# Expert outputs of a mixture-of-experts layer: the last expert's rows kept in a buffer of their own, the other pairs summed during its sends

## What is computed

```python
x = x + _L0_attn_ref(_layernorm(x), ...)
x = x + _L0_ffn_ref(_layernorm(x), Wr, W1, b1, W2, b2, fw1, fb1, fw2, fb2)   # 8 experts, top 2, capacity 1.25
x = x + _L1_attn_ref(_layernorm(x), ...)
x = x + _L1_ffn_ref(_layernorm(x), ...)
```

## Time and profile before

| | us |
|---|---|
| median of 3 runs (lowest, highest) | 1352.74 (1351.85, 1353.42) |
| the profiled execution, own time | 1354.45 |
| its span, first to last instruction | 1352.6 |
| expert layers, from the first load of slots to the last product | 370.6 to 510.5 |
| last send issued, first load of a pair issued | 518.67, 520.89 |
| last add of `combine` begins | 539.41 |
| first product of `retention` | 540.79 |

### The profile page before, as it was taken

How to read it: one execution, slowest core, us unless ns; L and a number is a source line. 1 busy time by engine, 2 the same in 40 slices (tenths; PEclk the granted TensorE clock), 3 DMA queues, 4 the chain that set the end, 5 groups by cost and what they waited for, 6 DMA issues and landing times. The chain is left out here.

```text
span 1352.6 us, 26534 instructions
## 1 busy us (share of the span) xinstructions
PE 1163.8 (86%) x7852; PEld 784.2 (58%) x7852; DVE 1041.3 (77%) x2666; ACT 887.5 (66%) x2317; POOL 857.2 (63%) x800
## 2 busy tenths in 40 slices
PE   7789999758589992896899999988969999999796
PEld 4335444335378882342577777765646767777464
DVE  6699999859779983574788888846558888887564
ACT  5534444346356550675799898977659989898673
POOL 0365656157626664315788788876568888888663
PEclk9899999869989996897999999999999999999999
DMA  4520000033212214200000000000000000000002
GB/s 134 209 74 1 1 1 1 1 100 107 64 65 74 74 54 140 67 0 24 1 2 2 1 0 1 0 1 1 0 25 2 2 2 0 1 0 1 1 1 63
DMA packets 35024, 44.00 MB, mean 33 GB/s; under 512 B 5621, under 2 KB 24978, under 8 KB 34913
## 3 DMA queue, kind: packets, MB, share of 16 engines
q1 hardware_dynamic: 30304, 34.27, 7.8%
q0 software_dynamic: 4608, 8.47, 1.9%
HBM read 22.65 MB, written 21.12 MB: 32 GB/s over the span
## 5 line engine op out<-in xcount | busy, mean ns | idle before, releaser
L2282 DVE TENSOR_TENSOR R<-bank,tab 128x1024 f32<-128x1024 f32 x128 | 156.0, 1224 | 68.1 <-ACT sq L2192 67.2
L2226 ACT ACTIVATE W<-W,nm 128x128 f32<-128x128 f32 x512 | 198.2, 393 | 0.4
L1980 POOL TENSOR_TENSOR R<-R 128x512 f32<-128x512 f32 x128 | 161.1, 1280 | 16.0 <-DVE R L2282 16.0
L2305 DVE CUSTOM_DVE_ANT_0 W<-bank,mask_q,rn 128x128 f32<-128x128 f32 x512 | 147.4, 344 | 18.4 <-PE bank L2101 13.5
L1995 POOL TENSOR_TENSOR W<-W,rden 128x512 f32<-128x512 f32 x128 | 132.4, 1040 | 41.0 <-DVE rden L2312 35.4
L1490 POOL DMA_INDIRECT expert_rows<-Yt,xin x80 | 82.7, 1034 | 67.8 <-DVE Yt L1463 50.1
L2226 ACT ACTIVATION_READ_ACCUMULATOR W<-W,nm 128x1 f32 x512 | 98.6, 193 | 0.0
L2210 ACT ACTIVATE QK<-bank 128x512 f32<-128x512 f32 x128 | 74.9, 585 | 35.4 <-PE bank L2076 34.1
L2101 PE MATMUL bank<-QK 64*64 64x128 f32 x2048 | 86.1, 283 | 3.4 <-DVE nm L2305 3.0
L2126 PE MATMUL bank<-PT,VA 128*64 128x128 f32 (+1 forms) x1024 | 85.9, 261 | 3.7 <-ACT PT L2234 2.7
L231 POOL DMA_INDIRECT expert_slots<-token_rows,dst x64 | 67.0, 1046 | 33.6 <-issue 18.8
(11 more groups left out here) (365 smaller groups left out, 3503.7 us busy)
## 6 DMA issues: line engine op xcount, KB each, us to landing
expert_slots<-empty SPq DMA_DIRECT2D x8, 650.0 KB, 6.3
xin<-expert_slots SPq DMA_DIRECT2D x8, 650.0 KB, 4.0
expert_rows<-empty SPq DMA_DIRECT2D x8, 512.0 KB, 6.8
token_rows<-expert_rows SPq DMA_DIRECT2D x16, 256.0 KB, 4.1
expert_raw<-w1e_dram SPq DMA_DIRECT2D x9, 256.0 KB, 2.9
expert_raw<-w2e_dram SPq DMA_DIRECT2D x9, 256.0 KB, 3.2
tok<-x_dram SPq DMA_DIRECT2D x8, 256.0 KB, 4.8
out_dram<-tok_out SPq DMA_DIRECT2D x8, 256.0 KB, 3.2
```

The costliest lines, as they stand in the source:

```text
L1980: nc.gpsimd.tensor_tensor(halves[:, :, 0, :, z, :], halves[:, :, 0, :, z, :], halves[:, :, 1, :, 1 - z, :], ALU.add).then_inc(summed, 1)
L2226: m = nc.scalar.activation(x, x, ACT.Exp, scale=-1.0, bias=nm[:, p % RING, j:j + 1], accum_out=den[:, p % RING, j:j + 1])
L2282: nc.vector.tensor_tensor(R[:, i, qk, :, :].rearrange("p c (h d) -> p c h d", d=DH), x, y.to_broadcast([P, 2, HEADS, DH]), ALU.mult).then_ ...
L2305: m = nc.vector.tensor_tensor_reduce(W[:, p % RING, j * P:(j + 1) * P], ps[BS[i]][:, cols], k.const["mask_q"][:, cols], rn[:, par, 2 * s + ...
```

## The change

- A new DRAM tensor `last_expert_rows` (`k.last`, 4096 rows). The last expert's outputs go there instead of into `k.ys`, by the plain token id, which is a third tail column (P + 2) of a row. A slot row grows from 520 to 524 bytes. The tensor is cleared at the same place as `k.ys`, with four more DMAs of 512 KB.
- In `expert_layers` SP waits for the sends of seven experts only and then loads all eight pairs, `load_first` into a buffer for each chunk and `load_second` into two buffers in turn. Before the third and each later `load_second` it waits for the sum that frees the buffer. DVE sums all eight pairs in this block.
- On DVE `weighted(i - 2)` moves from the end of turn i to the place after its second pair of roundings.
- In `combine` PE adds by products with the identity: 32 matmuls turn the sums of the pairs into the eight banks, 32 more add the last expert's rows, eight loads of 256 KB that SP issues once the last sends have landed. `transpose` becomes `matmul` with start and stop flags. POOL and DVE sum nothing there any more; DVE does the eight adds into `XT`.

```diff
-N_CLEAR = NE + 2 * T // (8 * P)
+N_CLEAR = NE + 3 * T // (8 * P)
...
+        self.last = nc.dram_tensor("last_expert_rows", (T, P), F32, kind="Internal").ap()
...
-ROW = P + 2
+ROW = P + 3
...
+                for q in range(T // (8 * P)):
+                    sp.dma_start(k.last[q * 8 * P:(q + 1) * 8 * P, :].rearrange("(p t) w -> p t w", p=P),
                                  empty[:, 0:8, 0:P]).then_inc(k.cleared, 16)
...
-                pool.wait_ge(tails, 2)
+                nc.gpsimd.tensor_copy(k.tok[:, 0:EARLY, P + 2:P + 3].rearrange("p n o -> p (n o)").bitcast(mybir.dt.uint32),
+                                      k.const["tokid"][:, 0, 0:EARLY]).then_inc(tails, 1)
+                pool.wait_ge(tails, 3)
...
-def load_pair(k, sp, Y, y_in, q):
-    for c in range(2):
-        rows = k.ys[c * T + q * CH:c * T + (q + 1) * CH, :].rearrange("(p t) w -> p (t w)", p=P)
-        sp.dma_start(Y[:, q % NPB, c, :], rows).then_inc(y_in[q], 16)
+def load_first(k, sp, Y, y_in, q):
+    rows = k.ys[q * CH:(q + 1) * CH, :].rearrange("(p t) w -> p (t w)", p=P)
+    sp.dma_start(Y[:, q, :], rows).then_inc(y_in[q], 16)
+
+
+def load_second(k, sp, Y, y_in, q):
+    rows = k.ys[T + q * CH:T + (q + 1) * CH, :].rearrange("(p t) w -> p (t w)", p=P)
+    sp.dma_start(Y[:, NCH + q % 2, :], rows).then_inc(y_in[q], 16)
...
+                for o in (P + 1, P + 2):
+                    i = V.tensor_copy(tok[:, cc, o:o + 1].rearrange("p n o -> p (n o)").bitcast(mybir.dt.uint32),
+                                      r["tokid"][:, 0, cc])
+                i.then_inc(routed, 1)
...
             for i, (t0, nt) in enumerate(EPARTS):
-                sp.wait_ge(sent[i], 16 * nt * NE)
-            for q in range(NPB):
-                load_pair(k, sp, Y, y_in, q)
+                sp.wait_ge(sent[i], 16 * nt * (NE - 1))
+            for q in range(NCH):
+                load_first(k, sp, Y, y_in, q)
+                if q > 1:
+                    sp.wait_ge(summed, q - 1)
+                load_second(k, sp, Y, y_in, q)
...
+            def add_pair(q):
+                dve.wait_ge(y_in[q], 32)
+                V.tensor_tensor(Y[:, q, :], Y[:, q, :], Y[:, NCH + q % 2, :], ALU.add).then_inc(summed, 1)
...
-                if i > 1:
+                        if i > 1 and j == 1:
+                            weighted(i - 2)
+                else:
+                    add_pair(i - S)
                     weighted(i - 2)
+            for q in range(2, NCH):
+                add_pair(q)
...
+                rows, column, back = (k.ys, P + 1, sent[s % 3]) if e < NE - 1 else (k.last, P + 2, last_sent)
...
         def _(sp):
-            for q in range(NPB, NCH):
-                sp.wait_ge(turned, q - NPB + 1)
-                load_pair(k, sp, Y, y_in, q)
+            sp.wait_ge(last_sent, 16 * CAP // P)
+            for q in range(NCH):
+                rows = k.last[q * CH:(q + 1) * CH, :].rearrange("(p t) w -> p (t w)", p=P)
+                sp.dma_start(L[:, q, :], rows).then_inc(y_in[q], 16)
...
+            def add_turned(q, rows, first):
+                for t in range(4):
+                    cols = slice(t * P, (t + 1) * P)
+                    m = nc.tensor.matmul(ps[q][:, cols], rows[:, q, cols], k.const["ident"][:], start=first and t == 0,
+                                         stop=not first and t == 3)
+                return m
+
             for q in range(NCH):
-                pe.wait_ge((summed_pool, summed_dve)[q % 2], q // 2 + 1)
-                for t in range(4):
-                    m = nc.tensor.transpose(ps[q][:, t * P:(t + 1) * P], Y[:, q % NPB, 0, t * P:(t + 1) * P], k.const["ident"][:])
-                m.then_inc(turned, 1)
+                add_turned(q, Y, True)
+            for q in range(NCH):
+                pe.wait_ge(y_in[q], 48)
+                add_turned(q, L, False).then_inc(turned, 1)
```

More of the change, by code:

```diff
@@ L1535, in add_residual @@
                 nc.vector.tensor_tensor(x, ps[q][:].rearrange("d (t p) -> d t p", t=4), x, ALU.add).then_inc(resid, 1)
-            for q in range(0, NCH, 2):
-                add_pair(q + 1)
-                add_residual(q)
-                add_residual(q + 1)
 def experts(k):
@@ L1548, in experts @@
         routing(k, w, wide, slots)
-        Y = k.rows[:].rearrange("p (a c w) -> p a c w", a=NPB, c=2)
-        expert_layers(k, w, wide, slots, Y, y_in)
-        combine(k, Y, y_in)
+        Y = k.rows[:].rearrange("p (a w) -> p a w", w=CH)
+        last_sent = big.enter_context(k.nc.semaphore("last_sent"))
+        expert_layers(k, w, wide, slots, Y, y_in, last_sent)
+        combine(k, Y, y_in, last_sent)
 SPLIT = ("wqkv",)
```

35 lines of the change are left out of this document (13 added, 22 removed).

## The result

The changed kernel takes 1358.6 us as a median of 15 runs, the kernel before beside it 1352.74 us: ratio 1.0043, 95% interval 1.0033 to 1.0052. A second measurement gave 1356.4 us against 1352.59 us, ratio 1.0049 (1.0027 to 1.0071). The forecast was 1353.1 us, no change, with 1357.2 us as the upper end of its range; the first measurement lies above it, the second inside.

A forecast was written before the change was run, and what follows sets the result against it. PE was taken to bound most of the expert layers, with only the tail movable. `combine` starting 3.55 us earlier but growing 3.9 us gave +0.4 us on 1352.74 us: 1353.1 us, range 1349.4 to 1357.2 us.

The forecast's parts named there:

- Step 1: Expert layers: `weighted` ahead of two rounding pairs brings sends forward, so SP begins pair loads at 505.55 us.
- Step 2: End of expert layers: pair loads and sums run under the sends; `combine` begins at 522.95 us, 3.55 us earlier.
- for a landing amid sends I take 2.9 us: Pair loads in the expert layers: 2.9 us per landing, from weight loads beside POOL's sends; bounds 2.5 and 4.1 us.
- rival A: Pair loads share DMA and land in 4.1 us; `combine` begins at 526.55 us, whole time 1356.7 us; chance 0.11.
- With 0.3 us for the barrier: Between the last pair sum at 522.65 us and `combine`: the barrier takes 0.3 us, so `combine` begins at 522.95 us.
- Step 3: `combine`: 64 identity products on PE instead of 32 transposes; takes 17.9 us instead of 13.96 us, 3.9 us longer.
- The second pass: `combine`, PE adding the last expert's rows: 0.88 us per chunk, DVE's adds 0.99 us apart being the later ones.
- The first pass: `combine`, PE turning pair sums: 64 pieces in 8.8 us, 16 at half clock in 3.5 us, the rest at full clock.
- B: `combine`: PE's clock stays at half, pieces 0.22 us, `combine` 29.5 us, whole time 1364.7 us; chance 0.06.
- E: `combine`: a product costs four transposes, 0.44 us at full clock; 31.2 us in all, whole time 1366.4 us; chance 0.02.
- C: Expert layers: `weighted` moves but POOL's sends don't come earlier; all 2.5 us later, 1355.6 us; chance 0.05.
- D: `retention`: PE still at full clock there, up to 3.2 us saved, 1349.9 us; chance 0.20 in full or in part.

The follow-up runs named there:

- kernel with own buffers: Changed kernel with a separate buffer for each second half, so no load waits for a sum; ratio 0.9980 to the kernel before, scattered.
- warm PE: Changed kernel with 90 idle transposes on PE in the expert-layer block, 18 behind each of pair sums 2 to 6; 1357.9 us, one run.
- one_block: Kernel before with `combine`'s instructions put into the expert-layer block, so no barrier lies between; ratio 0.9992 to the kernel before, scattered.
- sums in SBUF: Changed kernel with last rows added to pair sums in SBUF on POOL and DVE, and 32 transposes; ratios 0.9940 and 0.9898 to the kernel before, scattered.

## Why the prediction was wrong

**Step 1, `weighted` earlier: right.** (Times in this part are from the first profile unless another is named.) The first pair load was issued at 502.48 us, on the old clock (2.8 us more) 505.3 us, forecast 505.55 us. The sum of pair 0 began at 505.85, so 508.7 us, forecast 509.1 us. The last send began at 514.33, so 517.1 us, forecast 517.6 us.

**Step 2, the pairs: the landing was mis-sized, and a floor was left out.** The term "for a landing amid sends I take 2.9 us" failed: it measured 3.0 to 4.5 us, median 3.8 us (3.7 us in the second profile), and the odd chain ended at 522.6 instead of 519.9 us (522.65 us on the old clock). That is rival A, whose bound of 4.1 us was the one nearer to the truth. Its argument against itself, that only two loads queue after the change, was wrong: the first halves run beside the second ones and the sends, and DMA is 0.88 busy there. Without the sends a turn is still 3.6 to 4.5 us. But had I taken the right landing, or had the change removed the chain, the step would not have been mended, as the kernel with own buffers shows. The other sentence that failed is "With 0.3 us for the barrier": behind the sends the barrier opens no sooner than POOL's drain lets it, 6.6 us after the end of the last send. From the forecast's own last send, 517.6 + 0.98 + 6.6 + 0.1 = 525.3 us, the start of `combine` could gain 1.1 us, not 3.55 us. It gained 0.8 us in the first profile, where the chain of pairs was the last by 0.7 us, and 1.1 us in the second, where POOL's drain was. The stretch from 520.89 to 526.5 us, which I had read as "nothing but DMA", held two things side by side. POOL's drain ended at 526.24 us and opened the barrier. The loads of pair 1, for which DVE's first sum waits, were not much earlier, since in one block without the barrier this sum started no sooner behind S. Only POOL's sum of pair 0 was held up.

**Step 3, `combine`: right in kind, short by the clock.** The second pass and its adds took what they should, 7.31 us for 64 pieces (0.11 us each) and 8.0 us for eight adds. The first pass was forecast at 8.8 us with the clock rising after 3.5 us; it took 10.3 us with a rise after 6 us, and 8.75 us with a rise after 3 us. From barrier to barrier the forecast has 17.9 us and the barrier's few tenths, against 19.9 and 18.3 us.

**The sum.** Forecast: -3.55 us for the start, +3.9 us for `combine`, together +0.4 us. Measured: -0.8 and +5.6 us, together +4.8 us in the first profile; -1.1 and +4.0 us, together +2.9 us in the second. The medians say +5.9 and +3.8 us. So of the 4.4 us by which the first profile misses the forecast the start of `combine` has 2.8 us and the first pass at half clock 1.5 us; of the 2.5 us in the second profile the start has nearly all. About 1 us of either median's loss lies outside of this stage, and no run places it.

**The rivals.** A came true in part: the landings were long, and the barrier's floor that it left out lay just as late. B, half clock throughout, and E, a product at the price of four transposes, did not: pieces are 0.11 us apart in the second pass. C did not: the sends came earlier. D, PE fast into `retention`, did not in the first profile, whose first product there has 2.04 us; in the second it took 1.10 us and the next one 2.07 us again, so one product was won. The Trainium skill, "TensorE: Matmul & The Clock Gate", section "Why this matters for your kernels", asks for no long idle gaps of PE between bursts. The warm PE bears it out for the first pass (7.4 instead of 8.75 to 10.3 us), and the changed kernel is the case it warns of: PE is idle for 15.3 us and then the one engine that everybody waits for.

**What stays open.** Why the drain costs 6.6 us is not shown, only when. How the long landings divide between the sends and the other loads is not shown either. What the whole time makes of the gains by stage scatters by 2 to 3 us in the later layers. And on the scattered occasions the kernels that have `weighted` at the end of the turn ran the expert layers more slowly than the ones that have it early, 144.6 to 158.1 us (3 profiles) from the first turned input to E against 134.5 to 142.7 us (9 profiles); in calm both take 135.0 to 136.5 us. In the slowest PE waited 6.3 us in 100 for DVE's `weighted`, in the fastest not at all. No run was made to separate that from the clock. It may be one reason why the versions built on the changed kernel have lower ratios there than in calm.

## What to carry to other kernels

Before forecasting that a block ends sooner, find out which engine's drain opens its barrier, and what that drain hangs on: an engine that has done nothing for 6 us may be the last one in. Taking the barrier away helps only the work that was ready before it opened. Work that is moved ahead of a barrier wins only down to the next floor, while work that it leaves behind the barrier counts in full and, after an idle stretch of PE, at half clock. Price landings under load by the landings of loads that were under load, here the median of 4.1 us that already stood in the trace (3.8 us was measured), not by the nearest quieter ones.

## What the chip showed beside this

- POOL's drain at the end of a block that holds indirect DMAs ended 6.6 us behind POOL's last instruction in fifteen of the twenty profiles, ordinary POOL work between the last indirect DMA and the drain (`one_block`) included. It ended 6.05 us behind POOL's last wait where POOL had sat in waits for 8 us, and 5.1 us behind the 64 sends of `routing`, in all twenty. In `combine` of the kernel before, a block without indirect DMAs, it took 0.07 us.
- In four profiles the last send landed late, 3.3 to 3.9 us behind its end, and the drain ended 6.6 to 7.2 us behind the send, 3.30 us behind the landing in each (the first profile of the changed kernel, both with sums in SBUF, and the warm PE). (Landings are read from the semaphore records of the traces.) In the fifteen the landing was never later than 3.2 us behind the end of the last send. So both set a floor, and a late landing can raise it.
- PE, busy without a gap from idle, got the full clock after 3 us in one run of the same program and after 6 us in another.
- The time at half clock up to the expert layers differed between calm and scattered profiles by 24 to 67 us for nearly the same code, which hid effects of a few tenths of a per cent; stages counted from an event next to the change kept them readable to 1 us.
